# A three-block network on one core: rounding moved to ScalarE, spectral sums moved to VectorE, the convolution's steps set on a new timetable

## The chip, the cores and the metric

The kernel runs on one core of one Trainium2 chip. The metric is the device time in microseconds, from one launch to its end. TensorE is called PE here, VectorE DVE, ScalarE ACT, GpSimd POOL, and the queue on SyncE that issues the transfers SP. Each of them works through its own list of instructions in order; they meet at semaphores.

## The reference

The input is x, of 4 sequences by 1024 positions by 256 channels. Three blocks follow each other, each with a layer norm in front and a residual around it:

```python
x = x + 0.5 * ffn(layernorm(x))
x = x + attn(layernorm(x))
x = x + 0.5 * ffn(layernorm(x))

# ffn: all weights ternary, each layer followed by a scale per output channel
h = silu(x @ w1.T * s1) * (x @ w2.T * s2)      # 256 -> 1024
h = gelu(h @ h1.T * sh1)                       # 1024 -> 1024
h = gelu(h @ h2.T * sh2)                       # 1024 -> 1024
y = h @ w3.T * s3                              # 1024 -> 256

# attn: a long convolution along the sequence, by FFTs of length 2048
K = s4d_kernel(...)                            # taps, 256 channels x 1024
y = irfft(rfft(x, 2048) * rfft(K, 2048))[:1024]
y = gelu(y) @ W.T + b
```

## The kernel before

**Tiles.** The first feed-forward runs over 8 tiles of 512 tokens (T = 0 to 7), the second over 8 more (T = 8 to 15). A tile goes through 24 steps k: 0 to 7 make the gated product (`layer_one`), 8 to 15 the layer h1 and 16 to 23 the layer h2 (`hidden`); then come the transposes of the next tile's normed input and the last layer (`layer_three`). An activation is held as two float32r numbers, a rounded high part and the remainder (`hid_a_hi`, `hid_a_lo`, `hid_b_hi`, `hid_b_lo`), since float32r matmuls drop low bits and the ternary weights are exact in it. So a step of a hidden layer is 16 matmuls: 8 blocks of the input, high and low.

**One step of a hidden layer.** PE fills one of four PSUM banks. ACT applies the GELU and writes float32 to `act_o`, one of 3 slots (L567). DVE copies it rounded into the high part (L1178) and subtracts it from `act_o` into the low part (L1180). PE may refill the bank 4 steps later (it waits for ACT alone), and the next layer's first step waits block by block for the low parts. `layer_three` waits for ACT's last activation and then, block by block, for the low parts.

**The convolution** is spread over the same tiles, between the steps, by hand-written tests on T and k (`spectral` of each engine). The taps are made in T = 1 to 3: POOL makes phases and decays (L482, L491), DVE reduces the phases (`turn_steps`), ACT takes the sines (L609, with a table load ahead and one behind, since the steps around it use GELU), DVE multiplies (`table_step`, L873) and PE has 16 small matmuls a chunk (`tap_step`, L1304), one chunk every two steps. In T = 4 their spectrum is taken. Each sequence then has a pair of tiles: a *first* tile (T = 5, 7, 9, 11) and a *second* tile (T = 6, 8, 10, 12). In a first tile DVE folds the input into halves (`fold_*`, `rotate_*`), PE transforms the even half at k = 14 (`forward_even`), DVE multiplies by the taps' spectrum (`products` 0 to 3, from `ks`, two buffers that SP loads from DRAM), POOL adds pairs of products (`sums`, L497) and sums and differences of those (L534, L535), and PE transforms back at k = 21 (`inverse_even`, L1328 to L1334). In a second tile the odd half goes the same way: products 4 to 7, `gather_odd`, `gather_odd_again`, PE's `inverse_odd` at k = 15, `unrotate`, `join`, `transpose_y`, `project`. The layer norms sit at steps that `norm1_at` (for the next tile's input) and `norm2_at` (the norm ahead of the convolution) give; their inverse root is taken on POOL (`inverse_root`, L430).

**Order.** Nothing is scheduled by a program: the place of every instruction is the place where the tests on k put it, on each engine's own list.

Of the kernel before, what the change touches and what calls it, by code (L numbers as in the profile page):

```python
# [16 lines left out]
TILES = 2 * B  # L17
# [95 lines left out]
def norm1_at(T):  # L113

    if T == 0:
        return 13, 14
    if T == 1:
        return 13, 15
    if T in (2, 3):
        return 15, 17  # L120
    if T == 4:
        return 19, 20
    if first_of(T):
        return 18, 19
    if second_of(T):
        return 13, 14
    return 12, 13


def norm2_at(T):  # L130

    if T == 1:
        return 11, 12
    if T in (2, 3):
        return 11, 13
    if T == 4:
        return 18, 19
    return (20, 21) if 4 < T <= TILES else (-1, -1)
# [22 lines left out]
def build(nc, a, out):  # L161
    ctx = ExitStack()
    with ctx:
# [16 lines left out]
        def zone(start, *tensors):  # L180
# [62 lines left out]
        s_zt, s_zhi, s_zlo, s_u, s_act, s_gate, s_ghi, s_glo, s_hi, s_split, s_o, s_upd, s_x = (sem(n) for n in (  # L243
            "s_zt", "s_zhi", "s_zlo", "s_u", "s_act", "s_gate", "s_ghi", "s_glo", "s_hi", "s_split", "s_o", "s_upd",
# [6 lines left out]
        s_prod, s_y, s_pre, s_preo, s_wt, s_xc, s_bias = (sem(n) for n in (  # L251
            "s_prod", "s_y", "s_pre", "s_preo", "s_wt", "s_xc", "s_bias"))
# [30 lines left out]

        def product_home(i):

            if i % 2 == 0:
                return tt[:, 0:4]
            return zb[:, 4:8] if i < 4 else wb[:, 0:4]
# [132 lines left out]
        def _(pool):  # L421
# [72 lines left out]
            def sums(c, i):  # L494
                pool.wait_ge(s_prod, (c - 1) * 8 + i + 1)
                t = product_home(i)
                G.tensor_tensor(fb[:, spectrum_at(i)], t[:, 0:4:2], t[:, 1:4:2], ALU.add).then_inc(s_y, 1)  # L497

# [28 lines left out]
            for T in range(5, ALL):  # L527
                first, second = first_of(T), second_of(T)
                if first:
                    for i in range(4):  # L530
                        sums(first, i)
                    inverse_root("first", T + 1)
                    pool.wait_ge(s_y, (first - 1) * 8 + 4)
                    G.tensor_tensor(zb[:, 0:2], fb[:, 4:6], fb[:, 6:8], ALU.add)  # L534
                    G.tensor_tensor(zb[:, 2:4], fb[:, 4:6], fb[:, 6:8], ALU.subtract).then_inc(s_pre, 1)  # L535
                    if norm2_at(T)[0] >= 0:
                        inverse_root("second", T - 1)
                elif second:
                    for i in range(4, 8):
                        sums(second, i)  # L540
# [3 lines left out]
                    if norm2_at(T)[0] >= 0:  # L544
                        inverse_root("second", T - 1)
# [3 lines left out]
                    last.then_inc(s_bias, 1)  # L549
                else:  # L550
                    norms(T)

        @block.scalar
        def _(act):
            A = nc.scalar.activation

            def hidden(T, k, func, scale):
                act.wait_ge(s_u, at_u(T, k))
                if k < ACT_SLOTS:
                    if T:  # L560
                        act.wait_ge(s_split, at_split(T - 1, k + PER_U - ACT_SLOTS))
                elif k - ACT_SLOTS < KH:
# [48 lines left out]
            def copy_even(c):  # L611
                act.wait_ge(s_rb, c + 1)
                act.wait_ge(s_ef, c + 1)
                A(zb[:, 0:2], units(7), ACT.Copy).then_inc(s_cpe, 1)
# [6 lines left out]
            def scale_even(c):  # L621
                act.wait_ge(s_ei, c)
                A(tt[:, 0:2], units(7), ACT.Copy, scale=small[:, C_S4:C_S4 + 1])
                A(tt[:, 2:4], units(6), ACT.Copy, scale=small[:, C_S4:C_S4 + 1])
                A(zb[:, 4:6], units(5), ACT.Copy).then_inc(s_sce, 1)
# [21 lines left out]
            def spectral(T, k):  # L647
# [15 lines left out]
                if first and k == 16:  # L663
                    copy_even(first)
                if first and k == 21:
                    scale_even(first)
                if second and k == 14:
                    scale_odd(second)
                if second and k == 21:
                    gelus(second)  # L670
# [37 lines left out]
        def _(dve):  # L708
# [205 lines left out]
            def fold_third():  # L914
                marked()
                V.tensor_tensor(fb[:, 0:2], zb[:, 0:7:6], zb[:, 1:8:6], ALU.add)
                V.tensor_tensor(fb[:, 2:4], zb[:, 0:7:6], zb[:, 1:8:6], ALU.subtract)
                V.tensor_scalar(tt[:, 0:2], zb[:, 2:6:3], col(C_S4), None, ALU.mult)
                mark(V.tensor_scalar(tt[:, 2:4], zb[:, 3:5], col(C_S4), None, ALU.mult))

            def rotate(out0, out1, x0, x1, c_):

                V.scalar_tensor_tensor(out0, x0, c_, tt[:, 0:2], ALU.mult, ALU.subtract)
                return V.scalar_tensor_tensor(out1, x1, c_, tt[:, 2:4], ALU.mult, ALU.add)

            def rotate_quarter():
                marked()
                last = rotate(fb[:, 4:6], fb[:, 6:8], zb[:, 3:5], zb[:, 2:6:3], col(C_C4))
                last.then_inc(s_r4, 1)

            def rotate_eighth(j, n):
# [3 lines left out]
                marked()  # L935
                V.tensor_scalar(tt[:, 0:2], x1, col(C_SA + j), None, ALU.mult)
                mark(V.tensor_scalar(tt[:, 2:4], x0, col(C_SA + j), None, ALU.mult))
                marked()
                mark(rotate(zb[:, 2 * j:2 * j + 2], zb[:, 4 + 2 * j:6 + 2 * j], x0, x1, col(C_CA + j)))

            def rotate_odd(h):
                x0, x1 = (zb[:, 0:2], zb[:, 2:4]) if h == 0 else (zb[:, 6:8], zb[:, 4:6])
                marked()
                V.tensor_scalar(tt[:, 0:2], x1, col(C_S4), None, ALU.mult)
                mark(V.tensor_scalar(tt[:, 2:4], x0, col(C_S4), None, ALU.mult))
                marked()
                last = rotate(wb[:, 4 * h:4 * h + 2], wb[:, 4 * h + 2:4 * h + 4], x0, x1, col(C_C4))
# [5 lines left out]
            def spectrum_even(c):  # L953
                dve.wait_ge(s_cpe, c + 1)
                V.tensor_tensor(fb[:, 4:6], units(6), zb[:, 0:2], ALU.add)
                V.tensor_tensor(fb[:, 6:8], units(6), zb[:, 0:2], ALU.subtract).then_inc(s_xe, 1)
# [17 lines left out]
            def turn(i):  # L974

                if i == 0:
                    dve.wait_ge(s_ef, 1)
                if i >= 2:
# [15 lines left out]
            def products(c, i):  # L994
# [4 lines left out]
                if i >= 2:  # L999
                    dve.wait_ge(s_y, n - 1)  # L1000
# [3 lines left out]
                t = product_home(i).rearrange("p (h u) d -> p h (u d)", h=2)  # L1004
                V.tensor_tensor(t, x, k_, ALU.mult).then_inc(s_prod, 1)  # L1005
# [20 lines left out]
            def gather_odd(c):  # L1026
                dve.wait_ge(s_y, c * 8)
# [19 lines left out]
            def unrotate(j):  # L1047
# [3 lines left out]
                V.tensor_scalar(tt[:, 0:2], x, col(C_SA + j), None, ALU.mult)  # L1051
                mark(V.tensor_scalar(tt[:, 2:4], y, col(C_SA + j), None, ALU.mult))
                marked()
                last = rotate(fb[:, j:j + 7:6], fb[:, 2 + j:5 + j:2], y, x, col(C_CA + j))
# [23 lines left out]
            def spectral(T, k):  # L1078
# [27 lines left out]
                if first:  # L1106
# [10 lines left out]
                    if k in (14, 15):  # L1117
                        rotate_odd(k - 14)
                    if k == 16:
                        products(first, 0)  # L1120
                        products(first, 1)
                    if k == 17:
                        spectrum_even(first)
                        products(first, 2)
                    if k == 18:
                        products(first, 3)
                    if k == 22:
                        inverse_even(first)
                    if k == 23:
                        inverse_even_again(first)  # L1130
                if second:
                    if k == 8:
                        products(second, 4)
                        products(second, 5)
                    if k in (9, 10):
                        products(second, k - 3)
                    if k == 11:
# [3 lines left out]
                    if k == 15:  # L1141
                        inverse_odd(second)
                    if k in (16, 17):
                        unrotate(k - 16)
                    if k == 18:
                        join(second)
                    if k == 19:
# [26 lines left out]
            def split(T, k):  # L1174
# [3 lines left out]
                V.tensor_copy(hi[:, k % KH], source).then_inc(s_hi, 1)  # L1178
                dve.wait_ge(s_hi, at_split(T, k))
# [59 lines left out]
        def _(pe):  # L1239
# [112 lines left out]
            def inverse_even(c):  # L1352
# [3 lines left out]
                whole(6, C4, zb[:, 0:2])  # L1356
                whole(7, S4, zb[:, 2:4], s_ei)
# [32 lines left out]
            def spectral(T, k):  # L1390
# [10 lines left out]
                if first and k == 21:  # L1401
# [3 lines left out]
                if second and k == 22:  # L1405
# [90 lines left out]
```

## Time and profile before

| | |
|---|---|
| time before, median of 3 runs | 1565.17 us (1561.81 to 1567.83) |
| the profiled execution, its own time | 1559.97 us |
| its span, first to last instruction | 1558.2 us |
| mean granted clock of PE | 0.983 of full speed |
| PE busy | 1481.3 us, 95% of the span |
| DVE busy | 1058.7 us, 68% |
| ACT busy | 523.1 us, 34% |
| POOL busy | 265.2 us, 17% |

PE is the engine that works nearly without a pause, so the table is read from there: what moves the end is a time in which PE stands still or runs at a lower clock. The other engines' shares are averages; each of them can still be the one that PE waits for at a given place.

### The profile page before, as it was taken

Reading aid. Unit: us, or ns where it says so; the run is one execution under the profiler, and the core shown is the slowest. Engines: PE = TensorE matmul, PEld = TensorE weight load, DVE = VectorE, ACT = ScalarE, POOL = GpSimd, SP = SyncE. Lnnn points to the kernel's source line nnn. Section 1 sums busy time; section 2 is a strip of 40 time slices with the busy share of each in tenths; the row PEclk is TensorE's granted clock in tenths of the full one; section 3 lists DMA queues with packets and bytes.
Section 4 is the critical chain, followed back from the end, with each engine's and each line's share of the span. In section 5 each row is a group of like instructions: output and inputs, shape, how many; then the busy total and the mean of one; then the engine's idle time right before and its main releaser. Section 6 shows DMA issues by size and latency. Waiting matters only on the chain.

```text
span 1558.2 us, 17472 instructions
## 1 busy us (share of the span) xinstructions
PE 1481.3 (95%) x6910; PEld 1193.8 (77%) x6910; DVE 1058.7 (68%) x1689; ACT 523.1 (34%) x743; POOL 265.2 (17%) x245
## 2 busy tenths in 40 slices
PE   7598979989999999999999999999999999999998
PEld 3477867777788777878778787687876878888886
DVE  6598486977857777886778867777476774344432
ACT  5334235545542332422324232232322323232231
POOL 0014473744600002001021010210102101000000
PEclk9799999999999999999999999999999999999999
DMA  7100100000001322103121031221212211000000
GB/s 291 64 1 14 41 1 28 27 15 14 28 14 51 116 74 66 61 20 122 41 78 58 11 122 41 68 68 36 70 41 68 68 38 41 27 14 28 28 1 14
DMA packets 52114, 78.24 MB, mean 50 GB/s; under 512 B 2752, under 2 KB 44736, under 8 KB 50624
## 3 DMA queue, kind: packets, MB, share of 16 engines
q1 hardware_dynamic: 52032, 77.12, 14.7%
q8 instruction: 55, 0.90, 0.2%
q14 instruction: 27, 0.22, 0.0%
HBM read 56.14 MB, written 20.97 MB: 49 GB/s over the span
## 4 chain that ended last, share of the span: by engine, by line
PE 75%; DVE 10%; issue 8%; ACT 3%; POOL 2%; DMA 1%; DVEq 0%; POOLq 0%; ACTq 0%
PE ps L1255 59%; PE ps L1297 7%; PE ps L1334 3%; PE ps L1387 2%; PE ps L1304 2%; DVE hid_a_lo L1180 1%; ACT L609 1%; DVE hid_a_hi L1178 1%; DVE table L873 1%; ACT ph L609 1%; DMA ks<-k_d 1%; PE ps L1328 1%; DVE table L866 1%; DVE tt L1005 1%; PE ps L1329 1%
## 5 line engine op out<-in xcount | busy, mean ns | idle before, releaser
L567 ACT ACTIVATE act_o<-ps,scales 128x512 f32<-128x512 f32 x384 | 264.8, 690 | 965.2 <-PE ps L1255 961.5
L1255 PE MATMUL ps<-hid_a_hi,h 128*128 128x512 f32 x1024 | 409.8, 400 | 7.0 <-issue 6.0
L1255 PE MATMUL ps<-hid_b_hi,h 128*128 128x512 f32 x1024 | 405.3, 396 | 0.8 <-DVE hid_b_lo L1180 0.7
L1255 PE MATMUL ps<-hid_a_lo,h 128*128 128x512 f32 x1024 | 404.7, 395 | 0.0
L1255 PE MATMUL ps<-hid_b_lo,h 128*128 128x512 f32 x1024 | 402.0, 393 | 0.0
L1255 PEld LDWEIGHTS ps<-hid_a_hi,h 128*128 128x128 f32 x1024 | 194.5, 190 | 55.9 <-issue 8.2
L1255 PEld LDWEIGHTS ps<-hid_a_lo,h 128*128 128x128 f32 x1024 | 194.6, 190 | 43.6 <-issue 2.2
L1255 PEld LDWEIGHTS ps<-hid_b_hi,h 128*128 128x128 f32 x1024 | 192.6, 188 | 45.4 <-DVE hid_b_lo L1180 2.1
L1255 PEld LDWEIGHTS ps<-hid_b_lo,h 128*128 128x128 f32 x1024 | 192.6, 188 | 43.2 <-issue 1.2
L1255 PE MATMUL ps<-hid_b_hi,w 128*128 128x512 f32 x480 | 189.7, 395 | 2.4 <-DVE gz L1232 2.1
L1255 PE MATMUL ps<-hid_b_lo,w 128*128 128x512 f32 x480 | 188.6, 393 | 0.0
L1178 DVE CAST hid_b_hi<-act_o 128x512 fp32r<-128x512 f32 x128 | 63.1, 493 | 161.0 <-ACT act_o L567 160.0
L1178 DVE CAST hid_a_hi<-act_o 128x512 fp32r<-128x512 f32 x128 | 66.1, 516 | 144.9 <-ACT act_o L567 144.7
L1166 DVE SCALAR_TENSOR_TENSOR gz<-ps,scales,act_o 128x512 f32<-128x512 f32 x128 | 96.1, 751 | 67.3 <-ACT act_o L567 65.6
L1297 PE MATMUL ps<-w,hid_a_hi 128*128 128x256 f32 x512 | 126.1, 290 | 15.3 <-DVE hid_a_lo L1180 9.6
L1297 PE MATMUL ps<-w,hid_a_lo 128*128 128x256 f32 x512 | 122.2, 283 | 0.0
L1255 PEld LDWEIGHTS ps<-hid_b_hi,w 128*128 128x128 f32 x480 | 90.1, 188 | 33.7 <-DVE gz L1166 10.1
L1297 PEld LDWEIGHTS ps<-w,hid_a_hi 128*128 128x128 f32 x512 | 98.6, 193 | 18.9 <-DVE hid_a_lo L1180 10.5
L497 POOL TENSOR_TENSOR fb<-tt 128x512 f32<-128x512 f32 x16 | 25.3, 1583 | 496.4 <-DVE tt L1005 496.4
L1180 DVE TENSOR_TENSOR hid_a_lo<-act_o,hid_a_hi 128x512 fp32r<-128x512 f32 x128 | 103.2, 806 | 4.4
L430 POOL TENSOR_TENSOR rstd<-vare,expo 128x4 f32<-128x4 f32 x24 | 26.8, 1117 | 451.4 <-DVE vare L839 390.1
L1255 PEld LDWEIGHTS ps<-hid_b_lo,w 128*128 128x128 f32 x480 | 90.3, 188 | 16.1 <-issue 0.2
(227 smaller groups left out, 1698.9 us busy)
## 6 DMA issues: line engine op xcount, KB each, us to landing
ks<-k_d SPq DMA_DIRECT2D x32, 512.0 KB, 4.4
stages<-in_weights SPq DMA_DIRECT2D x9, 1024.0 KB, 5.0
gz<-in_x SPq DMA_DIRECT2D x8, 512.0 KB, 3.7
xin<-in_x SPq DMA_DIRECT2D x8, 512.0 KB, 3.9
x_d<-xin SPq DMA_DIRECT2D x8, 512.0 KB, 2.9
z_d<-xin SPq DMA_DIRECT2D x8, 512.0 KB, 2.9
k_d<-ks SPq DMA_DIRECT2D x8, 512.0 KB, 3.1
zb<-z_d SPq DMA_DIRECT2D x8, 512.0 KB, 5.6
```

Source lines behind the costliest of these rows:

```text
L430: G.tensor_tensor(rstd[:, :], vare[:, :], expo[:, :], ALU.pow).then_inc(s_rstd, 1)
L497: G.tensor_tensor(fb[:, spectrum_at(i)], t[:, 0:4:2], t[:, 1:4:2], ALU.add).then_inc(s_y, 1)
L567: A(act_o[:, k % ACT_SLOTS], bank(source), func, scale=scale).then_inc(s_act, 1)
L609: A(ph[:, c % 2], ph[:, c % 2], ACT.Sin, scale=TWO_PI_DOWN).then_inc(s_sin, 1)
L1166: V.scalar_tensor_tensor(gated[:, m % 2], bank(2 * (m % 2) + 1), scales[:, 1, m:m + 1], act_o[:, m % ACT_SLOTS], ALU.mult, ALU.mult).then_ ...
L1178: V.tensor_copy(hi[:, k % KH], source).then_inc(s_hi, 1)
L1180: V.tensor_tensor(lo[:, k % KH], source, hi[:, k % KH].bitcast(F32), ALU.subtract).then_inc(s_split, 1)
L1255: last = MM(o, weight[:, k, cols].bitcast(dt), part[:, k].bitcast(dt), start=(k == 0 and i == 0), stop=(k == n - 1 and i == len(act_) - 1))
L1297: last = MM(o, part[:, k, j * P:(j + 1) * P].bitcast(dt), w3[:, k].bitcast(dt), start=(k == 0 and i == 0), stop=(k == KH - 1 and i == 1))
L1304: last = MM(ps[:, 4 + i // 32, (i % 32) * 2 * A8:(i % 32 + 1) * 2 * A8], table[:, c % 2, i % CH, :], kp[:, i, 0:2 * A8], start=True, stop= ...
L1334: last = MM(bank(o), tables[:, table_], flat(x), start=True, stop=True)
L1387: last = MM(o, ga[:, k, u * P:(u + 1) * P], wt[:, k], start=(k == 0), stop=(k == KD - 1))
```

## The change

It has three parts.

1. **Rounding.** In the steps 8 to 23 ACT runs its activation twice from the same bank: first into the high part (float32r), then into `act_o` (float32). DVE's rounding copy goes, and with it the semaphore `s_hi`.
2. **Sums.** The sums of products, and the sums and differences ahead of `inverse_even`, move from POOL to DVE. The rotations keep their first terms in their own outputs instead of in `tt`, which leaves `tt` free for the products.
3. **Timetable.** In first tiles products 0 to 3 come at k = 14 to 17 (before: 16, 16, 17, 18), the rotation of the odd half at 18 and 19 (before: 14 and 15), `gather_even` at 18, `inverse_even` at 20 on PE (before: 21), the norms at 11, 12 and 19, 20. In second tiles the products come one a step at k = 8 to 11, `gather_odd` and what follows one step later, while `inverse_odd` on PE stays at 15.

```diff
     if first_of(T):
-        return 18, 19
+        return 11, 12
     if second_of(T):
-        return 13, 14
+        return 14, 15
...
                 source = 2 * (k % 2) if k < KH else k % 4
+                if k >= KH:
+                    A((hid_b_hi if k < 2 * KH else hid_a_hi)[:, k % KH], bank(source), func, scale=scale)
                 A(act_o[:, k % ACT_SLOTS], bank(source), func, scale=scale).then_inc(s_act, 1)
...
-                V.tensor_copy(hi[:, k % KH], source).then_inc(s_hi, 1)
-                dve.wait_ge(s_hi, at_split(T, k))
                 V.tensor_tensor(lo[:, k % KH], source, hi[:, k % KH].bitcast(F32), ALU.subtract).then_inc(s_split, 1)
...
-                V.tensor_tensor(t, x, k_, ALU.mult).then_inc(s_prod, 1)
+                V.tensor_tensor(tt.rearrange("p (h u) d -> p h (u d)", h=2), x, k_, ALU.mult).then_inc(s_prod, 1)
+                dve.wait_ge(s_prod, n + 1)
+                mark(V.tensor_tensor(fb[:, spectrum_at(i)], tt[:, 0:4:2], tt[:, 1:4:2], ALU.add))
+
+            def gather_even():
+                marked()
+                V.tensor_tensor(tt[:, 0:2], fb[:, 4:6], fb[:, 6:8], ALU.add)
+                V.tensor_tensor(tt[:, 2:4], fb[:, 4:6], fb[:, 6:8], ALU.subtract).then_inc(s_pre, 1)
...
                     if k in (14, 15):
-                        rotate_odd(k - 14)
+                        products(first, k - 14)
...
+                    if k in (18, 19):
+                        rotate_odd(k - 18)
                     if k == 18:
-                        products(first, 3)
+                        gather_even()
+                    if k == 21:
+                        inverse_even(first)
...
-                    if k == 12:
+                    if k == 13:
                         gather_odd_again()
...
-                if first and k == 21:
+                if first and k == 20:
                     inverse_even(first)
                 if second and k == 15:
                     inverse_odd(second)
```

ACT's list in tile 2, around one sine of the taps (`ph` is the phase). Before:

```order
L567 ACTIVATE act_o<-ps,scales 128x512
L609 ACT_TABLE_LOAD
L609 ACTIVATE ph<-ph 128x1024
L567 ACT_TABLE_LOAD
L567 ACTIVATE act_o<-ps,scales 128x512 x2
```

and with the change (L552 and L553 are the two activations, L595 the sine):

```order
L552 ACTIVATE hid_b_hi<-ps,scales 128x512
L553 ACTIVATE act_o<-ps,scales 128x512
L595 ACT_TABLE_LOAD
L595 ACTIVATE ph<-ph 128x1024
L552 ACT_TABLE_LOAD
L552 ACTIVATE hid_b_hi<-ps,scales 128x512
L553 ACTIVATE act_o<-ps,scales 128x512
```

One more activation stands ahead of the sine and its table load, and one more behind them.

DVE's list in a first tile from step 17 (product 3) on, up to the sums that `inverse_even` waits for. Before, the last of DVE's work for them is the product, and two norm steps follow:

```order
L1178 CAST hid_a_hi<-act_o 128x512
L1180 TENSOR_TENSOR hid_a_lo<-act_o,hid_a_hi 128x512
L1005 TENSOR_TENSOR zb<-fb,ks 128x1024
L831 BN_STATS stats<-gz 128x6 x4
```

With the change (L1157 is the low part, L982 the product, L984 its sum, L907 to L911 the rotation, L988 and L989 `gather_even`):

```order
L1157 TENSOR_TENSOR hid_a_lo<-act_o,hid_a_hi 128x512
L982 TENSOR_TENSOR tt<-fb,ks 128x1024
L984 TENSOR_TENSOR fb<-tt 128x512
L1157 TENSOR_TENSOR hid_a_lo<-act_o,hid_a_hi 128x512
L907 TENSOR_SCALAR wb<-zb,small 128x512
L908 TENSOR_SCALAR wb<-zb,small 128x512
L910 SCALAR_TENSOR_TENSOR wb<-zb,small,wb 128x512
L911 SCALAR_TENSOR_TENSOR wb<-zb,small,wb 128x512
L988 TENSOR_TENSOR tt<-fb 128x512
L989 TENSOR_TENSOR tt<-fb 128x512
```

The last low part of that list is step 18's: behind it four instructions of the odd half's rotation stand ahead of the two that PE waits for.

## Rows read from the trace of the kernel before

**Rows 1.** Waits of PE: line waited for, total us, times, longest.
```profile
PE ps L1328 <- POOL zb L535: 12.4, 4, 3.1
PE ps L1304 <- DVE table L873: 10.5, 14, 0.8
PE ps L1297 <- DVE hid_a_lo L1180: 9.6, 4, 3.5
PE ps L1297 <- ACT act_o L567: 5.7, 3, 4.3
```
**Rows 2.** Timeline of PE at `inverse_even`: tiles 7, 11 and 5.
```profile
800.40 1.22 PE L1328 MATMUL ps<-fb,tables 128*128 128x256 f32 x2 [3.10 <-POOL zb L535]
805.07 0.79 PE L1255 MATMUL ps<-hid_b_hi,h 128*128 128x512 f32 x1
...
1183.46 1.22 PE L1328 MATMUL ps<-fb,tables 128*128 128x256 f32 x2 [3.10 <-POOL zb L535]
1189.44 0.80 PE L1255 MATMUL ps<-hid_b_hi,h 128*128 128x512 f32 x1
...
610.43 0.70 PE L1328 MATMUL ps<-fb,tables 128*128 128x256 f32 x2 [3.09 <-POOL zb L535]
613.58 0.80 PE L1255 MATMUL ps<-hid_b_hi,h 128*128 128x512 f32 x1
```
**Rows 3.** Stages: PE busy, PEld, DVE, ACT, POOL, granted clock, DMA, GB/s.
```profile
800.40:802.00 1.60, 1.60 (x4) 1.33 (x5) 1.57 (x5) 0.00 (x0) 0.00 (x0) 0.50 0.00 0
542.00:546.00 4.00, 3.67 (x15) 2.72 (x16) 3.04 (x5) 1.56 (x3) 0.00 (x0) 1.00 0.80 285
```
**Rows 4.** Timeline, tile 7: ACT at steps 16, 18, 19; DVE's spectral forms.
```profile
782.41 0.69 ACT L567 ACTIVATE act_o<-ps,scales 128x512 f32<-128x512 f32 x1 [3.04 <-PE ps L1255]
783.00 0.59 ACT L614 ACTIVATE zb<-ps 128x512 f32<-128x512 f32 x1
...
789.88 0.69 ACT L567 ACTIVATE act_o<-ps,scales 128x512 f32<-128x512 f32 x1 [3.04 <-PE ps L1255]
793.61 0.69 ACT L567 ACTIVATE act_o<-ps,scales 128x512 f32<-128x512 f32 x1 [3.04 <-PE ps L1255]
...
780.48 0.48 DVE L944 TENSOR_SCALAR tt<-zb,small 128x512 f32<-128x512 f32 x1
782.06 0.75 DVE L924 SCALAR_TENSOR_TENSOR wb<-zb,small,tt 128x512 f32<-128x512 f32 x1
788.98 0.68 DVE L955 TENSOR_TENSOR fb<-ps,zb 128x512 f32<-128x512 f32 x1
```
**Rows 5.** Timeline around one tap chunk, tile 2.
```profile
272.94 0.69 ACT L567 ACTIVATE act_o<-ps,scales 128x512 f32<-128x512 f32 x1 [5.07 <-PE ps L1255]
274.95 1.06 ACT L609 ACTIVATE ph<-ph 128x1024 f32<-128x1024 f32 x1
277.32 1.96 PE L1304 MATMUL ps<-kp,table 128*128 128x16 f32 x16 [0.75 <-DVE table L873]
```
**Rows 6.** Chain of waits, tile 3: two steps behind tap chunks.
```profile
366.56 5.36 PE ps L1255 x16
378.28 3.79 PE ps L1255 x16
```
**Rows 7.** Timeline at the end of tile 15.
```profile
1544.72 0.39 PE L1297 MATMUL ps<-w,hid_a_hi 128*128 128x256 f32 x1 [0.78 <-ACT act_o L567]
```
**Rows 8.** Timeline at the end of tile 0, then tile 1.
```profile
129.39 0.39 PE L1297 MATMUL ps<-w,hid_a_hi 128*128 128x256 f32 x1 [3.03 <-DVE hid_a_lo L1180]
223.36 0.58 PE L1297 MATMUL ps<-w,hid_a_hi 128*128 128x256 f32 x1 [3.51 <-DVE hid_a_lo L1180]
```
**Rows 9.** Timeline of DVE in tile 1.
```profile
197.58 1.31 DVE L1178 CAST hid_a_hi<-act_o 128x512 fp32r<-128x512 f32 x1
```
**Rows 10.** Timeline of tile 6: gathering ahead of PE's `inverse_odd`.
```profile
673.89 1.22 DVE L1037 TENSOR_TENSOR fb<-wb 128x1024 f32<-128x1024 f32 x1
677.32 3.17 PE L1334 MATMUL ps<-fb,tables 128*128 128x512 f32 x7
```

More of the change, by code:

```diff
@@ L137, in norm2_at @@
         return 18, 19
-    return (20, 21) if 4 < T <= TILES else (-1, -1)
+    if first_of(T):
+        return (19, 20) if T <= TILES else (-1, -1)
+    return (21, 22) if 4 < T <= TILES else (-1, -1)
 def turned_at(T):
@@ L242, in build @@
         s_bn, s_mv, s_stat, s_rstd, s_z, s_z2 = (sem(n) for n in ("s_bn", "s_mv", "s_stat", "s_rstd", "s_z", "s_z2"))
-        s_zt, s_zhi, s_zlo, s_u, s_act, s_gate, s_ghi, s_glo, s_hi, s_split, s_o, s_upd, s_x = (sem(n) for n in (
-            "s_zt", "s_zhi", "s_zlo", "s_u", "s_act", "s_gate", "s_ghi", "s_glo", "s_hi", "s_split", "s_o", "s_upd",
+        s_zt, s_zhi, s_zlo, s_u, s_act, s_gate, s_ghi, s_glo, s_split, s_o, s_upd, s_x = (sem(n) for n in (
+            "s_zt", "s_zhi", "s_zlo", "s_u", "s_act", "s_gate", "s_ghi", "s_glo", "s_split", "s_o", "s_upd",
             "s_x"))
@@ L250, in build @@
             "s_of", "s_cpo", "s_ab", "s_oi", "s_sco", "s_inv", "s_yt", "s_tr", "s_g", "s_pj", "s_x2", "s_x2st"))
-        s_prod, s_y, s_pre, s_preo, s_wt, s_xc, s_bias = (sem(n) for n in (
-            "s_prod", "s_y", "s_pre", "s_preo", "s_wt", "s_xc", "s_bias"))
+        s_prod, s_pre, s_preo, s_wt, s_xc, s_bias = (sem(n) for n in (
+            "s_prod", "s_pre", "s_preo", "s_wt", "s_xc", "s_bias"))
         s_mir, s_l1k, s_turn, s_kfin = (sem(n) for n in ("s_mir", "s_l1k", "s_turn", "s_kfin"))
@@ L492, in doubles @@
                     pool.wait_ge(s_dbl, c * DBL + k + 1)
[L494 to L497, printed above, removed]
             inverse_root("first", 0)
@@ L528, in _ @@
                 first, second = first_of(T), second_of(T)
[L529 to L540, printed above, removed]
+                if second:
                     inverse_root("first", T + 1)
@@ L549, in _ @@
                     last.then_inc(s_bias, 1)
+                    if norm2_at(T)[0] >= 0:
+                        inverse_root("second", T - 1)
+                elif first:
+                    inverse_root("first", T + 1)
+                    if norm2_at(T)[0] >= 0:
+                        inverse_root("second", T - 1)
                 else:
@@ L611, in copy_even @@
             def copy_even(c):
-                act.wait_ge(s_rb, c + 1)
                 act.wait_ge(s_ef, c + 1)
-                A(zb[:, 0:2], units(7), ACT.Copy).then_inc(s_cpe, 1)
+                A(fb[:, 4:6], units(7), ACT.Copy).then_inc(s_cpe, 1)
             def copy_odd(c):
@@ L622, in scale_even @@
                 act.wait_ge(s_ei, c)
+                act.wait_ge(s_rb, c + 1)
                 A(tt[:, 0:2], units(7), ACT.Copy, scale=small[:, C_S4:C_S4 + 1])
@@ L662, in spectral @@
                             finish_taps(i)
-                if first and k == 16:
+                if first and k == 14:
                     copy_even(first)
-                if first and k == 21:
+                if first and k == 20:
                     scale_even(first)
-                if second and k == 14:
+                if second and k == 15:
                     scale_odd(second)
-                if second and k == 21:
+                if second and k == 22:
                     gelus(second)
@@ L916, in fold_third, with rotate @@
                 V.tensor_tensor(fb[:, 0:2], zb[:, 0:7:6], zb[:, 1:8:6], ALU.add)
[L917 to L924, printed above, removed]
+                mark(V.tensor_tensor(fb[:, 2:4], zb[:, 0:7:6], zb[:, 1:8:6], ALU.subtract))
+            def rotate(out0, out1, x0, x1, c_, s_):
+                V.tensor_scalar(out0, x1, s_, None, ALU.mult)
+                mark(V.tensor_scalar(out1, x0, s_, None, ALU.mult))
+                marked()
+                V.scalar_tensor_tensor(out0, x0, c_, out0, ALU.mult, ALU.subtract)
+                return V.scalar_tensor_tensor(out1, x1, c_, out1, ALU.mult, ALU.add)
             def rotate_quarter():
-                marked()
-                last = rotate(fb[:, 4:6], fb[:, 6:8], zb[:, 3:5], zb[:, 2:6:3], col(C_C4))
+                last = rotate(fb[:, 4:6], fb[:, 6:8], zb[:, 3:5], zb[:, 2:6:3], col(C_C4), col(C_S4))
                 last.then_inc(s_r4, 1)
@@ L943, in rotate_odd @@
                 marked()
[L944 to L947, printed above, removed]
+                last = rotate(wb[:, 4 * h:4 * h + 2], wb[:, 4 * h + 2:4 * h + 4], x0, x1, col(C_C4), col(C_S4))
                 if h:
@@ L954, in spectrum_even @@
                 dve.wait_ge(s_cpe, c + 1)
-                V.tensor_tensor(fb[:, 4:6], units(6), zb[:, 0:2], ALU.add)
-                V.tensor_tensor(fb[:, 6:8], units(6), zb[:, 0:2], ALU.subtract).then_inc(s_xe, 1)
+                V.tensor_tensor(fb[:, 6:8], units(6), fb[:, 4:6], ALU.subtract)
+                V.tensor_tensor(fb[:, 4:6], units(6), fb[:, 4:6], ALU.add).then_inc(s_xe, 1)
                 dve.wait_ge(s_xe, c + 1)
@@ L977, in turn @@
                     dve.wait_ge(s_ef, 1)
+                    dve.wait_ge(s_rb, 1)
                 if i >= 2:
@@ L1050, in unrotate @@
                 marked()
[L1051 to L1054, printed above, removed]
+                last = rotate(fb[:, j:j + 7:6], fb[:, 2 + j:5 + j:2], y, x, col(C_CA + j), col(C_SA + j))
                 if j:
@@ L1117, in spectral @@
                     if k in (14, 15):
-                        rotate_odd(k - 14)
+                        products(first, k - 14)
                     if k == 16:
-                        products(first, 0)
-                        products(first, 1)
-                    if k == 17:
                         spectrum_even(first)
                         products(first, 2)
+                    if k == 17:
+                        products(first, 3)
+                    if k in (18, 19):
+                        rotate_odd(k - 18)
                     if k == 18:
-                        products(first, 3)
+                        gather_even()
+                    if k == 21:
+                        inverse_even(first)
                     if k == 22:
-                        inverse_even(first)
-                    if k == 23:
                         inverse_even_again(first)
                 if second:
[L1132 to L1137, printed above, removed]
+                    if 8 <= k <= 11:
+                        products(second, k - 4)
+                    if k == 12:
                         gather_odd(second)
-                    if k == 12:
+                    if k == 13:
                         gather_odd_again()
-                    if k == 15:
+                    if k == 16:
                         inverse_odd(second)
-                    if k in (16, 17):
-                        unrotate(k - 16)
-                    if k == 18:
+                    if k in (17, 18):
+                        unrotate(k - 17)
+                    if k == 19:
                         join(second)
-                    if k == 19:
+                    if k == 20:
                         join_again()
@@ L1355, in inverse_even @@
                 quarters(5, S4, C4, (fb[:, 2], fb[:, 3]), None)
-                whole(6, C4, zb[:, 0:2])
-                whole(7, S4, zb[:, 2:4], s_ei)
+                whole(6, C4, tt[:, 0:2])
+                whole(7, S4, tt[:, 2:4], s_ei)
             def forward_odd(c):
@@ L1400, in spectral @@
                     forward_even(first)
-                if first and k == 21:
+                if first and k == 20:
                     inverse_even(first)
@@ L1404, in spectral @@
                     inverse_odd(second)
-                if second and k == 22:
+                if second and k == 23:
                     transpose_y(second)
```

18 lines of the change are left out of this document (3 added, 15 removed).

## The prediction, made before the changed kernel was run

> **What bounds the kernel now.** I read the busy shares first: PE works 1481.3 of 1558.2 us. So I went on to what PE waits for [rows 1]; each instance also stands in its timeline. Four waits matter. In each of the four first tiles (5, 7, 9, 11) PE stands 3.10 us ahead of `inverse_even`, until POOL has made the last difference. In tiles 2 and 3 it stands 0.75 us ahead of 14 of the 16 tap chunks, until DVE has multiplied by the sine. At tile ends it waits for ACT's last activation or DVE's last low part. Other waits of PE, at the start of the program, are untouched by the change.
>
> A pause costs more than its length where the clock falls after it. In tile 7 the eight transforms behind the pause take 805.07 - 800.40 = 4.67 us, in tile 11 5.98, in tile 5 only 613.58 - 610.43 = 3.15 [rows 2]. The granted clock right behind the pause of tile 7 is 0.50 of full speed, that is 1.2 GHz; behind a pause of 2.10 us at 540 us it stays 1.00, 2.4 GHz [rows 3]. Tap chunks do it too: twice in the 14, the step behind the chunk takes 5.36 us instead of 3.79 [rows 6].
>
> **The change part by part.** Times count from PE's end of a step, which is where ACT starts.
>
> *The second activation* costs ACT one start-to-start distance, 783.00 - 782.41 = 0.59 us, and DVE sees `act_o` that much later [rows 4]. DVE no longer copies (0.43 us when undisturbed, about 0.46 from start to start), so the low part is ready only about 0.12 later. In a plain step nobody waits for either: PE needs a bank again after four steps of 3.7 us. The shifted activation counts where something follows it at once:
>
> - The sine. The 0.75 us pause hangs on a chain from the activation at 272.94 over table load, sine (274.95) and DVE to PE at 277.32, without a gap [rows 5]. Everything in it moves by 0.59: 14 x 0.59 = **+8.3 us**. It could be nothing only if the sine did not stand behind both activations on ACT's list, and it does.
> - Tile ends. In tiles 3, 4, 13 and 14 the transposes end just as the activation does, in tile 15 PE waits 0.78 us for it [rows 7]; each moves by about 0.57: 5 x 0.57 = **+2.9 us**. In tiles 5 to 12 `forward_odd` or `project` stands between and hides it, up to 3 us and more.
> - The end of tile 2 hangs on sine, turn and low part: +0.59 for the sine, -0.46 for the copy, **+0.1**.
>
> *The copy that goes* pays where DVE is behind. At the end of tile 0 PE waits 3.03 us for the last low part [rows 8] and 0.28 ahead of that. DVE is busy without a break from step 17 there; six copies of 0.46 to 0.86 us go, 3.3 us of them usable, so the wait goes and the later activation (+0.57) is what remains: **-2.7 us** (between 0 and -3.3). At the end of tile 1 PE waits 3.51 us for the low part [rows 8] and 4.34 for an activation. There the copies take up to 1.31 us instead of 0.43, with POOL at work beside them [rows 9], but POOL's own chain of phase and decay sets when the first sine and the first table can be made. I take half a microsecond from the copy and a little from the turn: **-0.8** (between 0 and -6).
>
> *Even half ahead.* DVE's last work for `inverse_even` is now at step 18. From PE's end of step 18 (789.83 in tile 7, where ACT starts at 789.88 [rows 4]): `act_o` at +1.33, low part until +1.97, then, at DVE's distances of 0.39 to 0.75 for the forms of rows 4, the rotation (two of 0.48, two of 0.75: 2.33 together) and `gather_even` (two of 0.68: 1.29), with 0.05 for the semaphore: +5.65. PE is there after step 19, at +3.73, so it waits about 1.95 us where it waited 3.10: 4 x 1.15 = **-4.6 us**. The products are clear of it: each ks load has two steps, 7.4 us, where before a product waited for its load. The 32 sums on DVE fit into their steps of 3.7 us: a step holds a low part, a product and a sum, about 0.6 + 1.15 + 0.65 us. A pause of 1.95 is under the 2.10 that left the clock alone, so the clock losses of tiles 7, 9 and 11 go: 1.5 + 1.4 + 2.8 = **-5.7 us** (between 0 and that; 9's transforms took 4.53).
>
> *Odd half.* `gather_odd_again` moves to step 13 but PE's `inverse_odd` stays ahead of step 15's matmuls. In tile 6 PE starts it at 677.32, at once, and step 13 ended 3.67 before, at 673.6 [rows 10]. With the change: low part from +1.36, gathering from +1.97, two of 1.22 at a distance of 1.14, so the second ends at +4.33; PE waits 0.6: 4 x 0.6 = **+2.4 us** (0 to 3).
>
> *Moved without a price.* In tiles 6 and 8 POOL's second inverse root now stands behind two additions of 2.4 us that wait for a transfer; DVE's norm and the low part of step 23 then come some 5 us later, about 3 ahead of `layer_three`, which has the 6.9 us of `project` as cover. The residual's load starts 4.5 us later and still lands ahead of its use by 2 to 3 us. If that cover were gone it would cost 1 or 2 us, twice.
>
> *Clock in the tap stage.* A chunk keeps PE 1.96 us on 16-column matmuls behind 0.75 us of pause, and 2 of 14 were followed by a fall. With 1.34 us of pause the thin stretch is 3.3 us, of the length of the pauses of which 3 in 4 were followed by one. I take two falls more, 2 x 1.57 = **+3.2 us** (0 to 12 x 1.57 = 18.8).
>
> Sum: 8.3 + 2.9 + 0.1 - 2.7 - 0.8 - 4.6 - 5.7 + 2.4 + 3.2 = **+3.1 us** on the profiled execution's 1559.97. The median of the runs before is 5.2 above that execution, which I read as more such clock falls in a usual run, in the same places; so I add the sum to the median: 1565.2 + 3.1 = 1568.3, say **1568**.
>
> *A page weighed.* In tile 1, with POOL at work, a copy of DVE took 1.31 us [rows 9]; without POOL it takes 0.43. The Trainium skill, page "SBUF — State Buffer", section "SBUF: two separate sides", says that DVE and GpSimd take their shared port pair as an exclusive lock, held for a whole instruction, and that the other fully blocks. The trace agrees for DVE's side. By that, removing the copies frees POOL too, which would speak for the third rival below.
>
> **The rivals.**
>
> 1. *The clock falls at most tap chunks* (slower). Place: tiles 2 and 3. Price 1.57 us each. For it: the thin stretch grows to the length that had 3 falls in 4. Against it: 12 chunks with 2.7 us had none. With 9 or more added instead of 2: +3.1 + 11 = +14, 1579. It decides the sign beyond noise from 5 added falls on.
> 2. *No added fall*: +3.1 - 3.2, 1565. For it: in a chunk PE does work.
> 3. *Tile 1's end opens up*: POOL's chain shortens with DVE's copies gone, up to 5.2 us more, and 1.4 more since the matmuls there would not run at half clock: 1561 to 1562; with rival 2 as well 1558. Against it: POOL has the same list, and it starts only when the taps' factors are there.
> 4. *The second activation hides* at sine and tile ends: -8.3 - 2.9 - 3.2, 1554 (faster). Against it: the gapless chain.
> 5. *The change does not shorten the pause* ahead of `inverse_even`, because DVE comes to step 18 late: +4.6 + 5.7, 1578 (slower). Against it: DVE had 2 to 4 us to spare in steps 14 and 15.
>
> **How the numbers follow.** About 0.5%, 7.8 us, is what a measurement of this kernel can tell from no change. The forecast gets 0.45 (its own range 1562 to 1574), rival 1 0.22, rival 2 0.12, rival 3 0.09, rival 4 0.06, rival 5 0.06. Slower than 1573: rivals 1 and 5 and a little of the forecast, 0.29. Faster than 1557.3: rival 4, half of rival 3 with the small terms at their good ends, and a little of the forecast: 0.15. The rest, 0.56, is the same within 0.5%. The range takes in rival 3 and reaches rival 1: 1557 to 1580.
>
> **What would show it.** In the changed profile: PE waits ahead of L1304's counterpart 14 times 1.3 us (right) or 0.75 (rival 4); PE ahead of `inverse_even` four times 1.9 us, released by DVE's `gather_even`; PE ahead of `inverse_odd` four times 0.6; no wait for a low part at the end of tile 0; 3.3 to 3.5 us at the end of tile 1; `layer_three` of tile 15 1.4 us behind the last hidden matmul. The stages of tiles 2 and 3 show by their granted clock which of rivals 1 and 2 came. The prediction is wrong if PE's pauses in tiles 2 and 3 do not grow, if a wait of PE over 2 us stands where none is listed here, or if the matmuls themselves run at another pace.

## The result and the profile after

| | before | changed |
|---|---|---|
| median of 7 runs each | 1562.47 us (1558.71 to 1567.83) | 1576.09 us (1568.99 to 1581.69) |
| the profiled execution, its own time | 1559.97 us | 1581.69 us |
| span | 1558.2 us | 1579.9 us |
| PE busy | 1481.3 us | 1499.1 us |
| DVE, ACT, POOL busy | 1058.7, 523.1, 265.2 us | 923.8, 670.4, 208.4 us |

The ratio is 1.0072, 95% interval 1.0053 to 1.0091: slower, by some 11 us. The profiled execution of the changed kernel is its slowest run and that of before a fast one, so the two traces differ by 21.7 us. Where a length of time is read from them below, it explains these two executions; what the kernels cost in the mean is in the ratios.

First the waits of PE in the changed kernel (line, who released it, total us, times, longest), beside [rows 1]:

```profile
PE ps L1281 <- DVE table L859: 18.5, 14, 1.3
...
PE ps L1274 <- ACT act_o L553: 10.3, 8, 4.7
...
PE ps L1305 <- DVE tt L989: 7.7, 4, 1.9
...
PE ps L1274 <- DVE hid_a_lo L1157: 4.7, 3, 2.7
PE ps L1311 <- DVE fb L1021: 2.8, 4, 0.7
```

L1281 is the tap chunk (before 10.5 us), L1274 the last layer (before 5.7 and 9.6), L1305 `inverse_even` (before 12.4, released by POOL) and L1311 `inverse_odd`, a new wait. Added up, PE's idle time grew by only 3.9 us, 1579.9 - 1499.1 against 1558.2 - 1481.3. The rest, 17.8 us, is in PE's busy time: the same 6910 matmuls took longer.

Why, the stages show (us of the stage, then busy PE, PEld, DVE, ACT, POOL, the granted clock, DMA share, GB/s). First tiles 2 and 3 of the kernel before:

```profile
230.88:445.42 214.54, 200.54 (x1041) 165.89 (x1040) 160.03 (x216) 105.70 (x121) 101.92 (x115) 0.98 0.06 20
```

then of the changed kernel the same two tiles, 6 us of them, the place behind `inverse_even` of tile 7, and the start of tile 5:

```profile
226.63:466.35 239.72, 217.28 (x1041) 179.46 (x1040) 141.80 (x184) 124.19 (x153) 98.91 (x115) 0.91 0.06 18
398.00:404.00 6.00, 6.00 (x21) 5.13 (x21) 5.40 (x7) 0.44 (x1) 5.60 (x8) 0.50 0.00 0
818.00:822.00 4.00, 4.00 (x9) 2.55 (x9) 3.89 (x14) 0.00 (x0) 0.00 (x0) 0.59 0.00 0
562.00:566.00 4.00, 3.28 (x13) 2.43 (x14) 3.05 (x4) 1.87 (x4) 0.00 (x0) 1.00 0.79 296
```

The two tiles are 25.2 us longer, and their mean granted clock is 0.91, not 0.98. In stretches of 2 us each I find the clock at its lower level, 1.2 GHz, for 44 us of them in nine places, where before it was 7 us in two. Each of the nine places begins within 3.2 us of the start of a tap chunk that had a pause ahead of it. Behind `inverse_even` of tile 7 it is low again, though the pause ahead of it is now 1.93 us (3.10 before, [rows 2]); the same holds in all four first tiles. Behind the pause of 1.67 us at 562 us it stays at 2.4 GHz, as it did there before [rows 3]. What follows these pauses is not the same work: at 562 us PE goes on with products of 512 columns, behind the others come the transforms of `inverse_even` or a tap chunk of 16 columns.

By tile, from one final product of the last layer to the next, the changed trace minus that of before: tile 0 -5.3 us, tile 1 +1.0, tile 2 +11.7, tile 3 +13.5, tile 4 +0.2; first tiles 5, 7, 9, 11 -0.3, -1.0, -1.1, -2.7; second tiles 6, 8, 10, 12 +0.9 to +1.0 each; tiles 13 to 15 +0.5 to +0.9.

The chain ahead of a tap chunk, ACT's part of it in the changed kernel (start, us, engine, line), beside [rows 5]:

```profile
259.19 0.69 ACT L552 ACTIVATE hid_b_hi<-ps,scales 128x512 fp32r<-128x512 f32 x1 [6.08 <-PE ps L1232]
259.78 0.68 ACT L553 ACTIVATE act_o<-ps,scales 128x512 f32<-128x512 f32 x1
260.48 1.28 ACT L595 ACT_TABLE_LOAD   x1
261.77 1.06 ACT L595 ACTIVATE ph<-ph 128x1024 f32<-128x1024 f32 x1
```

The second activation starts 0.59 us behind the first, and the table load and the sine move by just that. PE's chunk follows at 264.14 after a pause of 1.32 us; it takes 2.92 us instead of 1.96, since the clock falls within it, and the step behind it 6.01 instead of 3.79.

### The profile page after: what moved, and what is told of

It is laid out like the page before. It is cut to its first block, busy times and chain, and to the rows that moved or that the text cites. A ratio compares the mean times of both kernels' runs of the same rounds, so it can differ in the third digit from the quotient of the medians.

```text
span 1579.9 us, 17462 instructions
## 1 busy us (share of the span) xinstructions
PE 1499.1 (95%) x6910; PEld 1208.2 (76%) x6910; DVE 923.8 (58%) x1473; ACT 670.4 (42%) x999; POOL 208.4 (13%) x205
## 4 chain that ended last, share of the span: by engine, by line
PE 82%; DVE 7%; ACT 4%; issue 3%; POOL 2%; DMA 1%; SPq 0%; ACTq 0%; POOLq 0%; DVEq 0%
PE ps L1232 66%; PE ps L1274 7%; PE ps L1311 3%; PE ps L1281 2%; PE ps L1364 2%; ACT act_o L553 1%; ACT L595 1%; DVE table L859 1%; ACT ph L595 1%; PE ps L1305 1%; PE ps L1306 1%; DVE hid_a_lo L1150 1%; DMA small<-in_small 1%; DVE hid_a_lo L1157 0%; PE ps L1223 0%
## 5 line engine op out<-in xcount | busy, mean ns | idle before, releaser
L1232 PE MATMUL ps<-hid_b_hi,h 128*128 128x512 f32 x1024 | 409.6, 400 | 0.0
L1232 PE MATMUL ps<-hid_b_lo,h 128*128 128x512 f32 x1024 | 406.3, 397 | 0.0
L553 ACT ACTIVATE act_o<-ps,scales 128x512 f32<-128x512 f32 x384 | 262.8, 685 | 224.7 <-PE ps L1232 224.7
L552 ACT ACTIVATE hid_b_hi<-ps,scales 128x512 fp32r<-128x512 f32 x128 | 88.4, 691 | 326.3 <-PE ps L1232 325.8
L1157 DVE TENSOR_TENSOR hid_b_lo<-act_o,hid_b_hi 128x512 fp32r<-128x512 f32 x128 | 89.5, 699 | 225.7 <-ACT act_o L553 225.7
L552 ACT ACTIVATE hid_a_hi<-ps,scales 128x512 fp32r<-128x512 f32 x128 | 88.4, 690 | 306.5 <-PE ps L1232 306.1
L1157 DVE TENSOR_TENSOR hid_a_lo<-act_o,hid_a_hi 128x512 fp32r<-128x512 f32 x128 | 95.3, 747 | 210.3 <-ACT act_o L553 206.3
L1274 PE MATMUL ps<-w,hid_a_hi 128*128 128x256 f32 x512 | 127.2, 292 | 15.0 <-ACT act_o L553 10.3
L1274 PE MATMUL ps<-w,hid_a_lo 128*128 128x256 f32 x512 | 123.5, 285 | 0.0
L1274 PEld LDWEIGHTS ps<-w,hid_a_hi 128*128 128x128 f32 x512 | 99.6, 195 | 18.8 <-ACT act_o L553 12.4
```

The lines of the kernel that those rows point to most:

```text
L552: A((hid_b_hi if k < 2 * KH else hid_a_hi)[:, k % KH], bank(source), func, scale=scale)
L1157: V.tensor_tensor(lo[:, k % KH], source, hi[:, k % KH].bitcast(F32), ALU.subtract).then_inc(s_split, 1)
L1232: last = MM(o, weight[:, k, cols].bitcast(dt), part[:, k].bitcast(dt), start=(k == 0 and i == 0), stop=(k == n - 1 and i == len(act_) - 1))
L1274: last = MM(o, part[:, k, j * P:(j + 1) * P].bitcast(dt), w3[:, k].bitcast(dt), start=(k == 0 and i == 0), stop=(k == KH - 1 and i == 1))
```

## The experiments

All are timed against the kernel before on the same chip; its medians there are 1565.55 us beside the first four and 1564.18 beside the last four. Each trace was also read for PE's waits and for the time at the lower clock in tiles 2 and 3.

**The first part alone.** ACT's second activation on the kernel before (and two waits of DVE on its own earlier rotation, which are met when it comes to them):

```diff
 # kernel before
+if k >= KH:
+    A((hid_b_hi if k < 2 * KH else hid_a_hi)[:, k % KH], bank(source), func, scale=scale)
 A(act_o[:, k % ACT_SLOTS], bank(source), func, scale=scale).then_inc(s_act, 1)
...
-V.tensor_copy(hi[:, k % KH], source).then_inc(s_hi, 1)
-dve.wait_ge(s_hi, at_split(T, k))
```

> The kernel before with the first part of the change alone: ACT writes the rounded part itself, DVE's copy is gone; sums stay on POOL and the timetable is the old one. Theory (the sine chain): PE's pause ahead of 14 tap chunks goes from 0.75 to 1.33 us, PE waits 0.5 to 0.6 us longer at the ends of tiles 3, 4, 13, 14, 15, the end of tile 0 gains some 3 us, and in tiles 2 and 3 the clock falls 5 to 9 times more at 1.6 us each. Pause ahead of inverse_even 3.1 us as before, no pause ahead of inverse_odd. Together +16 us (+12 to +22) on the time before. Rival (the timetable and the sums on DVE are what costs): this kernel stands within 3 us of the time before, and tiles 2 and 3 are no longer than before.

Measured: 1580.73 us, ratio 1.0109 (1.0080 to 1.0138), the whole loss of the change and some more. Its waits and tiles 2 and 3:

```profile
PE ps L1306 <- DVE table L875: 18.5, 14, 1.3
PE ps L1330 <- POOL zb L535: 11.5, 4, 3.0
...
225.78:464.03 238.25, 215.86 (x1041) 178.38 (x1040) 141.87 (x184) 124.08 (x153) 98.91 (x115) 0.91 0.06 18
```

The tap chunks pause as in the changed kernel and the clock is low for 41 us. So the loss is this part's; the other two parts have no share in it.

**The other two parts alone.** The changed kernel with DVE's copy back:

```diff
 # changed kernel
-if k >= KH:
-    A((hid_b_hi if k < 2 * KH else hid_a_hi)[:, k % KH], bank(source), func, scale=scale)
...
+V.tensor_copy(hi[:, k % KH], source).then_inc(s_hi, 1)
+dve.wait_ge(s_hi, at_split(T, k))
```

> The changed kernel with its first part undone: DVE copies the rounded part again, sums on DVE and the new timetable stay. Theory (the sine chain): tap chunks pause 0.75 us again, with 2 or 3 clock falls in tiles 2 and 3; the pause ahead of inverse_even is 1.8 us, ahead of inverse_odd 0.5 us; -1.3 x 4 + 0.5 x 4 = -3 us, so 1559 to 1562 where the kernel before has 1562.5. Rival (the timetable costs): 5 us or more above the time before.

Measured: 1560.36 us, ratio 0.9971 (0.9949 to 0.9993), a small gain as expected. Its waits on the tap chunks and in the convolution:

```profile
PE ps L1281 <- DVE table L857: 10.5, 14, 0.8
...
PE ps L1305 <- DVE tt L987: 7.3, 4, 1.9
...
PE ps L1311 <- DVE fb L1019: 2.3, 4, 0.6
```

**DVE's copy back in tiles 2 and 3 alone.**

```diff
 # changed kernel
-if k >= KH:
+if k >= KH and T not in (2, 3):
     A((hid_b_hi if k < 2 * KH else hid_a_hi)[:, k % KH], bank(source), func, scale=scale)
...
+if T in (2, 3):
+    V.tensor_copy(hi[:, k % KH], source).then_inc(s_hi, 1)
+    dve.wait_ge(s_hi, (T - 2) * 2 * KH + (k - KH) + 1)
```

> The changed kernel with DVE's copy put back in tiles 2 and 3 alone, where the tap chunks are. Theory: the 14 pauses are 0.75 us again (-8 us) and most of the clock falls there go (-6 to -14 us in the mean), the rest is as in the changed kernel: 1557 to 1562, where the changed kernel has 1576. If only the pauses counted and not the clock: 1567. Rival (the second activation costs wherever it stands): it keeps more than half of the loss, 1569 or more.

Measured: 1556.36 us, ratio 0.9955 (0.9934 to 0.9976), a little under what was expected. Against the changed kernel's 1.0072 that is 18 us from these two tiles, of which the pauses are 8. The low clock there went from 44 to 17 us. Outside these tiles the second activation costs nothing on balance: this kernel is no slower than the one with DVE's copies everywhere (0.9971).

**The two sums ahead of the rotation.**

```diff
 # changed kernel
-if k in (18, 19):
-    rotate_odd(k - 18)
 if k == 18:
     gather_even()
+if k in (18, 19):
+    rotate_odd(k - 18)
```

> The changed kernel with the two sums ahead of inverse_even placed ahead of the rotation at step 18 instead of behind it; the same instructions. The two sums then end 1.97 + 1.29 = 3.3 us behind step 18, before PE comes at 3.73. Theory: the four pauses of 1.93 us go (-7.7 us), and with them the four clock falls of 3.4 us at half clock behind them (another -5 to -6): 1562 to 1564. Rival (the clock falls in first tiles come from the light transforms themselves, not from the pause): the pauses go and the falls stay, 1568. Rival (another wait takes over, the rotation's outputs for forward_odd): no gain, 1576.

Measured: 1563.43 us, ratio 0.9985 (0.9965 to 1.0005), 13.6 us under the changed kernel. PE has no wait ahead of `inverse_even` any more, and behind it, in tile 5, the clock is whole:

```profile
619.00:623.00 4.00, 4.00 (x15) 2.66 (x15) 3.96 (x9) 0.21 (x1) 0.00 (x0) 1.00 0.00 0
```

Tiles 7, 9 and 11 take 92.5 us instead of 96.4 to 96.5 and tile 5 takes 94.1 instead of 98.6: 4.0 to 4.5 us each, where the pause was 1.93. The other half is the clock: in this trace no stretch at the lower level lies in tiles 5 to 15, but for the last 4 us of the program, in which PE has nothing to do. The transforms alone do not bring it down, a pause of 1.9 us ahead of them does. The other traces agree: of the kernels with a pause of 1.8 to 2.0 us there (the changed one and those of three experiments) all 16 places have a fall, of the three kernels with no pause none of 12. The tap stage, where nothing was moved, has 34 us at the lower clock in this trace and 44 in that of the changed kernel, so a single trace says what the clock costs only to some 5 us.

**A delay ahead of the sine, with nothing of the change.**

```diff
 # kernel before
 act.wait_ge(s_red, c + 1)
+A(scratch_512, constant_512, ACT.Copy)
 A(ph[:, c % 2], ph[:, c % 2], ACT.Sin, scale=TWO_PI_DOWN).then_inc(s_sin, 1)
```

(`scratch_512` is memory of `ks` that nothing reads, `constant_512` the identity read four times over.)

> The kernel before with nothing of the change, but one more activation of 512 elements (a copy of a constant into unused memory) on ACT ahead of each sine of the taps. Theory (a longer pause ahead of the chunk, whatever makes it, brings the clock falls): the 14 pauses grow from 0.75 to about 1.3 us (+7.5 us), and the stretches at half clock in tiles 2 and 3 go from 2 or 3 in a profile to 6 or more (+5 to +14 us): 1576 to 1584 beside 1563 to 1565 for the kernel before. Rival (the falls in the changed kernel came from its doubled activations or from DVE's other load): the pauses grow and the stretches stay at 2 to 4: 1571 to 1573.

Measured: 1582.10 us, ratio 1.0122 (1.0094 to 1.0149), as slow as the first part alone. Its pauses and tiles 2 and 3:

```profile
PE ps L1307 <- DVE table L876: 17.4, 14, 1.3
...
231.60:470.27 238.67, 217.36 (x1041) 179.28 (x1040) 156.96 (x215) 113.33 (x136) 100.87 (x115) 0.91 0.06 18
```

The low clock there is 44 us, with DVE's copies in place and each bank read once. So with the same chunk behind it, it is the pause's length that does it, whatever makes the pause.

**The tap chunks one step later on PE.** ACT's copy of the finished taps in tile 3 moves with them, from step 22 to 23; that edit is not shown.

```diff
 # changed kernel
-c = turned_at(T).get(k - 2) if k > KH else turned_at(T - 1).get(PER_U - 2)
+c = turned_at(T).get(k - 3) if k > KH + 1 else turned_at(T - 1).get(PER_U - 2) if k == KH + 1 else None
 if c:
     tap_step(c - 1)
-if T == 3 and k == 22:
+if T == 3 and k == 23:
     tap_step(SUBS - 1)
```

> The changed kernel with PE's 16 matmuls of each tap chunk one step later, so that the sine has a whole step more; nothing else is moved but ACT's copy of the finished taps in tile 3 (step 23 instead of 22). Theory: all 14 pauses of 1.33 us go (-18.5 us) and the clock falls of tiles 2 and 3 with them (-8 to -18): 1540 to 1549. Rival (the 16-column matmuls are what the clock falls on, pause or not): pauses go, falls stay: 1556 to 1558. Rival (DVE or POOL becomes the bound of the tap stage, whose two steps hold 7 to 8 us of DVE): a new wait, on DVE's turn steps or on the low parts, takes back more than 5 us.

Measured: 1543.55 us, ratio 0.9869 (0.9842 to 0.9896). All 14 pauses are gone, and against the changed kernel that is 31.8 us by the ratios, where the pauses were 18.5:

```profile
225.98:433.43 207.45, 199.84 (x1041) 169.29 (x1040) 144.65 (x184) 124.13 (x153) 101.53 (x115) 0.97 0.07 21
```

The low clock in the two tiles is 14 us, in two places, and both lie behind a new wait, of 2.5 us, at step 16 of tiles 2 and 3; here tile 2's, and what DVE did ahead of it:

```profile
283.00 0.50 PE L1232 MATMUL ps<-hid_b_hi,h 128*128 128x512 f32 x1 [2.47 <-DVE hid_b_lo L1157]
...
276.84 1.23 DVE L859 TENSOR_TENSOR table<-ph,dec 128x1024 f32<-128x1024 f32 x1 [1.73 <-POOL dec L487]
...
278.76 2.29 DVE L852 TENSOR_SCALAR table<-table,small 128x1024 f32<-128x1024 f32 x1
...
282.23 0.72 DVE L1157 TENSOR_TENSOR hid_b_lo<-act_o,hid_b_hi 128x512 fp32r<-128x512 f32 x1
```

POOL's decay is late for the table, and the low part of step 15 stands behind table and turn steps. Of the 16 chunks, 14 have no wait near them and no fall behind them. The other two stand 0.6 us behind the new wait, and there the clock falls, in tile 3 at 389.4 us:

```profile
387.72 0.50 PE L1232 MATMUL ps<-hid_b_hi,h 128*128 128x512 f32 x1 [2.46 <-DVE hid_b_lo L1157]
388.05 0.39 PE L1232 MATMUL ps<-hid_b_lo,h 128*128 128x512 f32 x1
388.28 2.44 PE L1281 MATMUL ps<-kp,table 128*128 128x16 f32 x16
```

So the 16-column matmuls alone do not bring the clock down. Whether a wait alone would, with no light work near it, this run does not show.

**All three moves together**: the two above, and `gather_odd_again` at step 12.

```diff
 # changed kernel, beside the two moves above
 if k == 12:
     gather_odd(second)
-if k == 13:
     gather_odd_again()
```

> The changed kernel with three moves: the two sums of the even half ahead of the rotation, the tap chunks one step later on PE, and gather_odd_again at step 12 together with gather_odd (so the pause of 0.7 us ahead of inverse_odd goes as well). Theory, by adding what each was found or expected to give: 1576 - 13 - 27 - 3 = 1533 (1527 to 1540), faster than the kernel before by 1.5 to 2.5%. Rival (the moves overlap, and what one gives the other already had): 1545 or more.

Measured: 1526.90 us (1525.50 to 1531.54), ratio 0.9766 (0.9741 to 0.9791), 2.3% under the kernel before and the fastest that was run. The expectation by adding was 1533 (1527 to 1540), and the result lies at its lower edge. Added up in measured ratios, the moves fit: 1.0072, less 0.0087 for the sums and 0.0203 for the chunks, less 2.8 us (0.0018) of pause ahead of `inverse_odd`, is 0.9764. PE's larger waits behind the start are these:

```profile
PE ps L1273 <- ACT act_o L553: 9.0, 8, 4.8
...
PE ps L1231 <- DVE hid_b_lo L1156: 4.9, 2, 2.5
PE ps L1273 <- DVE hid_a_lo L1156: 4.3, 2, 2.7
```

**The same, with DVE's copy** in all tiles (the edits of the second experiment and of this one).

> The same three moves, but with DVE making the rounded part as in the kernel before. Theory: with the sine off PE's path the second activation costs only 0.6 us at five tile ends and gives some 3 to 4 us back in tiles 0 and 1, so both ways of rounding stand within 4 us of each other: 1530 to 1540. Rival (DVE's copies, 127 us of its time, matter once the pauses are gone): this kernel is 5 us or more slower than the one with ACT's rounding.

Measured: 1538.24 us, ratio 0.9842 (0.9817 to 0.9868), 11.3 us slower than with ACT's rounding. My theory said within 4 us; its rival was right. DVE is now the bound at the places that are left:

```profile
PE ps L1273 <- DVE hid_a_lo L1156: 9.6, 4, 3.7
...
PE ps L1231 <- DVE hid_b_lo L1156: 7.5, 3, 3.6
```

Tile 0 ends at 135.1 us with the copies and at 130.9 without, and tiles 2 and 3 take 213.8 us instead of 206.3, with 24 us at the lower clock instead of 10.

## Why the prediction came out as it did

The time lay in the range of 1557 to 1580, and the sign was right: 1568 was said, +3 us, and it became 1576.09, +11 (ratio) to +14 (medians). It lay outside the forecast's own 1562 to 1574, and a change too small to tell from none, which was given 0.56, is not what came. The range holds the result only because it was drawn out to reach rival 1, so the hit is in part luck. The forecast also stood on a median of 3 runs that was 2.7 us above that of 7, which made its miss look smaller. The pauses were forecast rightly, term by term; of the two terms for the clock one was mis-sized and one was wrong, both to the same side.

- **The sine chain**, +0.59 us on each of 14 pauses: right. 18.5 us of pause against 10.5 is 8.0, 8.3 was said. The first part alone has the same 18.5.
- **Tile ends**: +0.48 us in tiles 3, 4, 13 and 14, 1.36 instead of 0.78 in tile 15: 2.5 us, 2.9 was said.
- **End of tile 0**: the two pauses of together 3.3 us became 0.86, -2.5; -2.7 was said. I had also said that no wait for a low part would be left; 0.37 of the 0.86 us is one. The tile is 5.3 us shorter in all, since a pause of 0.7 us at step 16 goes too and the clock was low for 3.4 us less after the start; over the ten kernels here it is about 5 us shorter without DVE's copies (130.4 us in the mean, not 135.4), and only part of that was in my sum.
- **End of tile 2**: its two waits went from 3.34 to 3.41 us, +0.07; +0.1 was said.
- **End of tile 1**: the wait for the low part went from 3.51 to 2.66 us, -0.85 as in the sum (my list of signs said 3.3 to 3.5, which does not go with it); but the one for the activation grew by 0.41, since both activations of step 23 wait behind the first sine and its table loads. My term left that out, and the clock was low for 14 us there and not 7, so the tile came out 1.0 us longer. The copies before took up to 2.14 us in this stretch, more than the 1.31 that I read; all the same the third rival, in which it opens up, did not come.
- **`inverse_even`**: 1.93 us of pause where 1.95 was worked out. Right.
- **`inverse_odd`**: 0.70 us where 0.6 was worked out, four times. Right.
- **The clock behind `inverse_even`**: wrong. I wrote that a pause of 1.95 is under the 2.10 that left the clock alone, "so the clock losses of tiles 7, 9 and 11 go", -5.7 us. The clock fell in all four first tiles. One place at which it had not fallen was no bound, and it was of another kind: behind the 2.10 us PE went on with products of 512 columns, not with the transforms. At that place, the start of tile 5, all ten kernels have a pause of 1.3 to 2.1 us and none has a fall; ahead of `inverse_even` 1.9 us were enough every time. Nor did 3.10 us bring a fall each time: it was three of four before. Both traces have some 13.7 us at the lower clock there, so the term is 0 and not -5.7. What it is worth, the experiment with the sums ahead shows: about 2 us in each of the four tiles beside the pause.
- **The clock in the tap stage**: mis-sized. I took two falls more, +3.2 us; it was seven places more, several of them twice as long as the two before. The profiled execution has 37 us more at the lower clock there, which at half speed is up to 18.7 us; by the tiles, 25.2 us less 8 of pause is 17. In the mean it is less: undoing the second activation in these two tiles gave 18 us in the ratios, less 8.1 of pause is 10. This is my first rival, which I gave 0.22, and it explains why the change is slower by more than noise and not by 3 us. My signs of being wrong had "if the matmuls themselves run at another pace": in the trace they did, by the clock alone, for 17.8 us.

The two clock terms together: I put -2.5 us; the traces say +17 for these two executions and the experiments about +10 in the mean. With the 3.9 us of added idle time that gives 14, the upper end of the +11 to +14 of the runs. The pauses alone were forecast to a few tenths each.

What stays open is how a pause is turned into a fall. Four traces here have the longer pause (1.2 to 1.33 us) ahead of 14 chunks: 9, 9, 9 and 8 of them have a fall behind them, and not the same ones from trace to trace. I tried two lengths there, 0.75 and 1.3 us, and zero, and no others. Nor did any run change the work behind a pause and leave its length, so that light work behind the pause is needed for a fall is only suggested by the start of tile 5.

## What to carry to other kernels

On an engine that works without a pause, count each wait twice: once for its length, and once for the clock it may cost; here the second part was 0.7 to 1.3 times the first (5.9 us beside 7.7 of pause ahead of `inverse_even`, 13 beside 18.5 for the moved chunks, 10 beside 8.1 for the sine chain). A spectral or table-making step that the bound engine reads should be one step further ahead than the mean of the others' busy shares suggests: moving two short groups of instructions past each other, and the 16 matmuls of each chunk by one step, each gave about 1.7 times what its pauses measured. And an instruction put on an idle engine is not free where a chain passes through that engine: ACT was 34% busy, and 0.59 us on it came out on PE 14 times.

## What the runs showed of the hardware that was not expected

- PE's clock fell to 1.2 GHz behind the pauses of 1.93 us ahead of `inverse_even` four times in four, and behind 9 of the 14 of 1.33 us ahead of the tap chunks; with a pause of 0.75 us ahead of the same chunks there were 2 to 4 such places among 14, with no wait near them none. Behind the pauses of 1.3 to 2.1 us at the start of tile 5, which products of 512 columns follow, it fell in none of ten traces.
- Two activations from the same bank start 0.59 us apart, though each is listed with 0.69 us, as the prediction had taken it; a table load followed by its first activation takes 1.29 us from start to start (260.48 to 261.77), and no more.
